# Edge units of an attention layer in two groups of three instead of three groups of two, one table set for exponential and logarithm, and a small chain of work spread over more groups

## The chip, the core and the metric

The kernel runs on one core of a Trainium2 chip. That core has TensorE (PE, matrix multiplication; its weight loads are listed as PEld), VectorE (DVE), ScalarE (ACT), GpSimd (POOL) and a queue engine (SP) that issues transfers. Each runs its own list of instructions in order, and they wait for one another on semaphores. The metric is the device time of one launch in microseconds (us).

## The reference

Four layers in a row on an input of 4 images of 16 x 16 places and 192 channels, all in 32-bit floating point. Layers 0 and 2 are attention blocks (normalise, windowed attention with relative positions, projection, normalise, two-layer perceptron with GELU). Layers 1 and 3 are spectral layers. Only the attention is touched here. Its core, for each window of 14 x 14 places:

```python
xp = pad(norm(x))                      # 16 x 16 -> 28 x 28, four windows per image
q, k, v = split(xp_windows @ qkv_w + qkv_b)          # 12 heads of 16 channels
attn = (q * scale) @ k.T + rel_h[..., :, None] + rel_w[..., None, :]
out = softmax(attn) @ v
out = (out @ proj_w + proj_b)[:, :16, :16]
```

Since 16 = 14 + 2, each image has one full window and three windows that consist mostly of padding. Only the 2-wide strips of them are real. Padded places have a zero input, so their keys are the bias of the key projection: a query in such a window sees its few real keys, and for all the padding three folded keys with a logarithm of a sum of exponentials as their weight.

## The kernel before

The two attention layers (l = 0 and 1 in the program) run the same code. The 12 heads are held in 3 slots of 4 heads. Places are in two kinds of groups:

- a *main* group is a slot and an image: 196 queries and 196 keys, the keys in two tiles of 128;
- an *edge* group is a slot and the strips of all images. The right strips (e = 0) and the lower strips (e = 1) are 120 queries each, with 120 real and 3 folded keys. A pair of slot and strip is called a unit here; there are six, and an edge group has two.

`GROUPS` (L254) lists 15 groups: 0 to 3 are slot 0 of the four images, 4 to 7 slot 1, 8 to 10 the edges of slots 0 to 2, and 11 to 14 slot 2 of the four images. The written order is a pipeline over them. In step n TensorE does, in interleaved quarters (loop at L1090),

- `turn(n)` (L1034): the scores of group n with keys on the partitions, heads 0 and 1 first (pair 0), then heads 2 and 3 (pair 1). ScalarE takes the exponential (`probsT`, L1398);
- `score(n + 2)` (L1006): the scores of a later group with queries on the partitions, from which VectorE takes each query's largest (`take_max`, L1585) and turns it (L1596); SP carries it by four transfers into the row of the relative positions that `turn` reads later;
- `weigh(n - 1)` (L1054) after half of pair 1: probabilities times values, with the sums of the probabilities.

`score(h)` waits until the largest of the half before last has been taken, because it writes the same banks. `turn(n)` waits for the exponentials of group n - 1 and for `pv_out` of group n - 2, since weighed results share bank 4 with the turned scores.

After the weighing, ScalarE copies the result out (`take_weighed`, L1385), which from the third group on waits until GpSimd has finished group n - 2 (the buffers are two deep). VectorE turns the sums and inverts them (`sum_up`, `spread`, L1606 to L1618; in its list two steps later), and GpSimd multiplies (`divide`, L808 to L821): for slot 2 straight to its place, for slot 0 by way of a part that is masked, for slot 1 by way of a mask and an addition. The edge results go to four pieces of the target, so each step of it is four instructions. `out_project` (L892) of image b waits for the division of group 11 + b (10 + b in the new numbering).

The folded keys' logarithms are made by a chain over three engines, which begins with the relative rows: VectorE turns them (`turn_rows`, L1624) and takes largest values (L1631); GpSimd subtracts (`shift_pads`, L785); ScalarE takes the exponential (L1403); VectorE adds up (L1637); ScalarE takes the logarithm (L1406); VectorE adds the largest back (`log_pads`, L1642); GpSimd fills three rows (`pad_rows`, L791); VectorE turns all back (L1647). GpSimd's own order is: edge inputs of slot 0, `shift_pads`, edge inputs of slot 1, `pad_rows`, then `divide(0)`, `divide(1)`, edge inputs of slot 2, `divide(2)` and on.

ScalarE holds one set of function tables at a time. A table load is its own instruction, before L1406 and again before the exponential that follows.

## Time and profile before

| | us |
|---|---|
| median of 3 runs (lowest to highest) | 334.32 (333.93 to 335.57) |
| the profiled execution | 337.13 |
| its span, first to last instruction | 335.3 |
| PE busy | 319.6 (95%) |
| PEld busy | 239.4 (71%) |
| DVE busy | 190.3 (57%) |
| ACT busy | 143.7 (43%) |
| POOL busy | 102.0 (30%) |
| mean granted TensorE clock | 0.98 of full |

```profile
PEclk9599998999999999999999999799999999999999
```

### The profile page before, as it was taken

What the parts mean: (1) busy time and instruction counts of PE and PEld (TensorE: products, weight loads), DVE (VectorE), ACT (ScalarE), POOL (GpSimd) and SP (SyncE); (2) the same over time, 40 slices, a digit from 0 to 9 for tenths busy, and PEclk for the clock granted to TensorE, in tenths of its full rate; (3) what the DMA queues carried; (4) which work ended last, traced back from release to release, by engine and by line L of the source; (5) the groups of instructions that cost most, each with busy time, mean ns of one, the idle gap of its engine ahead of it and who ended that gap; (6) DMA issues with size and microseconds to landing.
All of it is one profiled execution on the core that took longest, in us unless ns stands there. A gap on an engine that the chain in (4) does not pass through costs nothing.

```text
span 335.3 us, 9323 instructions
## 1 busy us (share of the span) xinstructions
PE 319.6 (95%) x3886; PEld 239.4 (71%) x3886; DVE 190.3 (57%) x457; ACT 143.7 (43%) x312; POOL 102.0 (30%) x215
## 2 busy tenths in 40 slices
PE   6999997999998999999999999799999899999997
PEld 3447686887876439977855769578887644998576
DVE  4473784877867400136674578587785920335572
ACT  3277136554556522024247515655455455002430
POOL 3000553487551049100000066277663104000000
PEclk9599998999999999999999999799999999999999
DMA  7973000000031103020021100000000000000002
GB/s 203 383 269 68 15 7 16 8 10 5 5 86 43 25 0 118 2 70 2 0 96 20 37 4 12 14 9 6 5 4 3 3 0 0 2 0 2 0 2 94
DMA packets 10268, 13.81 MB, mean 41 GB/s; under 512 B 3505, under 2 KB 8337, under 8 KB 10226
## 3 DMA queue, kind: packets, MB, share of 16 engines
q1 hardware_dynamic: 9602, 13.12, 12.5%
q8 instruction: 31, 0.51, 0.7%
q10 hardware_dynamic: 624, 0.09, 0.2%
q14 instruction: 11, 0.09, 0.1%
HBM read 10.95 MB, written 0.79 MB: 35 GB/s over the span
## 4 chain that ended last, share of the span: by engine, by line
PE 86%; DVE 7%; ACT 4%; DMA 2%; issue 1%; ACTq 0%; DVEq 0%
PE banks L1034 13%; PE banks L1006 12%; PE banks L1128 10%; PE banks L1146 9%; PE banks L962 6%; PE banks L1054 6%; PE banks L925 6%; PE banks L896 3%; PE banks L1312 2%; PE banks L885 2%; PE banks L1159 2%; PE banks L1206 2%; PE banks L938 2%; DMA slot_cols<-in_slot_cols 2%; ACT arena L1398 1%; PE banks L1176 1%
## 5 line engine op out<-in xcount | busy, mean ns | idle before, releaser
L1398 ACT ACTIVATE arena<-banks 128x392 f32<-128x392 f32 (+1 forms) x120 | 50.0, 469 | 44.0 <-PE banks L1034 44.0
L1585 DVE TENSOR_REDUCE negmax<-banks 128x4 f32<-128x784 f32 (+1 forms) x52 | 46.7, 897 | 17.5 <-PE banks L1006 17.0
L1006 PE MATMUL banks<-attention_arena 32*128 32x196 f32 x384 | 50.7, 365 | 0.9 <-DVE negmax L1581 0.4
L1034 PE MATMUL banks<-attention_arena 32*128 32x196 f32 x384 | 48.8, 351 | 0.4 <-ACT arena L1398 0.4
L1034 PE MATMUL banks<-attention_arena,keys 32*128 32x196 f32 x384 | 45.7, 332 | 0.0
L1006 PE MATMUL banks<-keys,attention_arena 32*128 32x196 f32 x384 | 45.5, 331 | 0.0
L1034 PEld LDWEIGHTS banks<-attention_arena 32*128 32x128 f32 x384 | 31.5, 191 | 7.0 <-issue 5.2
L1128 PE MATMUL banks<-yT,fc 128*128 128x512 f32 (+1 forms) x96 | 33.3, 607 | 0.0
L1006 PEld LDWEIGHTS banks<-keys,attention_arena 32*128 32x128 f32 x384 | 33.0, 190 | 0.0
L1034 PEld LDWEIGHTS banks<-attention_arena,keys 32*128 32x128 f32 x384 | 33.0, 190 | 0.0
L1006 PEld LDWEIGHTS banks<-attention_arena 32*128 32x128 f32 x384 | 29.9, 190 | 3.7 <-DVE negmax L1581 1.9
L1146 PEld LDWEIGHTS banks<-fc,arena 128*128 128x128 f32 x192 | 31.1, 190 | 1.5 <-ACT arena L1418 1.5
L756 POOL COPY edge_rel<-attention_arena 128x64 f32<-128x64 f32 (+1 forms) x24 | 4.3, 236 | 91.5 <-DVE attention_arena L1571 91.5
L1146 PE MATMUL banks<-fc,arena 128*128 128x192 f32 x192 | 31.7, 327 | 0.0
L1687 DVE TENSOR_TENSOR x_tok<-banks,x_plus_bias 128x384 f32<-128x384 f32 x8 | 4.5, 558 | 46.2 <-PE banks L1146 46.2
L1054 PE MATMUL banks<-arena,v_and_ones 128*32 128x196 f32 (+1 forms) x480 | 25.2, 328 | 4.7 <-ACT arena L1398 4.6
L1128 PEld LDWEIGHTS banks<-yT,fc 128*128 128x128 f32 (+1 forms) x96 | 12.8, 188 | 17.9 <-issue 15.4
L925 PE MATMUL banks<-yT,qkv 128*128 128x512 f32 (+1 forms) x48 | 21.6, 675 | 1.0 <-DVE yT L1504 1.0
L1054 PEld LDWEIGHTS banks<-arena,v_and_ones 128*32 128x32 f32 (+1 forms) x480 | 12.2, 109 | 13.4 <-ACT arena L1398 9.1
L962 PE MATMUL banks<-attention_arena,rel 32*32 32x192 f32 x512 | 21.2, 321 | 0.0
L1418 ACT ACTIVATE arena<-banks,cols 128x512 f32<-128x512 f32 x24 | 14.7, 687 | 14.9 <-PE banks L1128 14.9
L811 POOL TENSOR_TENSOR divided_part<-o_and_sums,inverse_sums 128x196 f32<-128x196 f32 (+1 forms) x20 | 12.4, 620 | 26.2 <-DVE inverse_sums L1618 26.2
(181 smaller groups left out, 583.2 us busy)
## 6 DMA issues: line engine op xcount, KB each, us to landing
fc<-in_fc SPq DMA_DIRECT2D x2, 768.0 KB, 5.0
fc<-in_fc SPq DMA_DIRECT2D x2, 576.0 KB, 5.6
attention_arena<-negmaxT SPq DMA_DIRECT2D x68, 1.0 KB
rel<-in_rel SPq DMA_DIRECT2D x2, 448.0 KB, 5.9
x_tok<-in_x SPq DMA_DIRECT2D x4, 192.0 KB, 4.4
inverse<-in_inverse SPq DMA_DIRECT2D x1, 768.0 KB
inverse<-in_space_back SPq DMA_DIRECT2D x1, 768.0 KB, 3.9
qkv<-in_qkv SPq DMA_DIRECT2D x1, 576.0 KB, 3.8
```

The lines of the kernel that those rows point to most:

```text
L811: pool.tensor_tensor(part, o, inverse, ALU.mult).then_inc(s.divided, 1)
L896: last = mm(m.bank[out_bank(b)][:, CH * tile:CH * (tile + 1)], m.oT[:, part, at:at + 128], wl["proj"][:, part], start=part == 0, stop=part ...
L925: ins = mm(bank[:, :], wl["qkv"][rows, half, 128 * g:128 * (g + 1)], m.yT[rows, half, 512 * part:512 * (part + 1)], start=not short, stop= ...
L962: ins = mm(bank[row(quad), 192 * n:192 * (n + 1)], wl["rel"][row(quad), 0 if kind == "rel_h" else 1, at % WIN], q[:, :, :, at], start=True ...
L1006: ins = mm(o, asking, asked, start=not with_rel, stop=bool(with_rel))
L1034: last = mm(m.bank[4 + j][key_rows(b), cols * tile:cols * (tile + 1)], keys_of(slot, b, j, tile)[with_rel], queries_of(slot, b, j, tile)[w ...
L1054: last = mm(m.bank[weighed_in(n)][row(j), out_at], values_of(slot, b, j, tile), m.probsT[key_rows(b), n % P_RING, j, cols * tile:cols * (t ...
L1128: ins = mm(m.bank[j % 8][:, :], wl["fc1"][rows, half, 128 * hid:128 * (hid + 1)], m.yT[rows, half, 512 * g:512 * (g + 1)], start=not short ...
L1146: last = mm(m.bank[4 + b][:, CH * tile:CH * (tile + 1)], m.hidT[:, hid, at:at + 128], wl["fc2"][:, hid], start=hid == 0, stop=hid == HID_T ...
L1398: run(m.probsT[keys, n % P_RING, j, 0:cols], m.bank[4 + j][keys, 0:cols], ACT.Exp).then_inc(s.probs, 1)
L1418: run(m.hidT[:, hid, 512 * g:512 * (g + 1)], m.bank[j % 8][:, :], ACT.Gelu, bias=wl["cols"][:, hid:hid + 1])\
L1585: dve.tensor_reduce(at[rows, 4 * part:4 * part + 4].rearrange("k (j a) -> k j a", a=2), m.banks[rows, 2 * part:2 * part + 2, 0:2 * keys].r ...
```

## The change

Line numbers of the new kernel are 26 to 53 higher. There are four parts.

1. The six units are in two edge groups of three (`PER_GROUP`): slot 0 both strips and slot 1 right strip; slot 1 lower strip and slot 2 both strips. There are 14 groups; 8 and 9 are edges. An edge group has 6 steps of `turn` and of `score` where it had 4, exponentials of 360 columns where it had 240, 12 multiplications in `weigh` where it had 8. All buffers for it grow to three units.
2. ScalarE loads one named table set after L1370's work, in which both exponential and logarithm are; no load stands around the logarithm.
3. The folded keys' chain moves in the written order. On VectorE `turn_rows` and the largest come after `take_max(5)`, the sums after `take_max(9)`, `log_pads` after `take_max(11)`, the turn back to step 4. On ScalarE its exponential follows group 1 (it followed group 0), and the logarithm group 2 (it followed group 1). GpSimd's order is as it was.
4. The semaphore of two small loads at the start is split: TensorE's first transposes wait for `ident` alone, not for `slot_cols` too.

```diff
-PAD_BLOCKS = SLOTS * 2 * 4
+UNITS = 2 * SLOTS
+PER_GROUP = 3
+PAD_BLOCKS = UNITS * 4
-GROUPS += [(slot, EDGES) for slot in range(SLOTS)]
+GROUPS += [(third, EDGES) for third in range(UNITS // PER_GROUP)]
+def units(n):
+    return range(PER_GROUP * GROUPS[n][0], PER_GROUP * (GROUPS[n][0] + 1))
+def key_tiles(b):
+    return 2 if b < EDGES else PER_GROUP
+def steps_of_group(n):
+    return 2 * key_tiles(GROUPS[n][1])
...
+                def divide_edges(n, ring):
+                    o, part, inverse = by_units(m.o[:, ring]), by_units(m.part[:, ring]), by_units(m.inverse[:, ring])
                     pool.tensor_tensor(part, o, inverse, ALU.mult).then_inc(s.divided, 1)
                     pool.wait_ge(s.divided, divided(n))
+                    for at, u in enumerate(units(n)):
+                        slot, e = divmod(u, 2)
+                        if slot == 1:
+                            ins = pool.tensor_scalar(part[:, at], part[:, at], masked(slot), None, ALU.mult)
+                            continue
+                        for to, of in zip(pieces(m.oT[:, slot // 2], e), in_pieces(part[:, at], e)):
+                            ins = pool.tensor_scalar(to, of, masked(slot), None, ALU.mult)
+                    ins.then_inc(s.divided, 1)
                     pool.wait_ge(s.divided, divided(n) + 1)
+                    at, u = [(at, u) for at, u in enumerate(units(n)) if unit_slot(u) == 1][0]
+                    for to, of in zip(pieces(m.oT[:, 0], u % 2), in_pieces(part[:, at], u % 2)):
                         ins = pool.tensor_tensor(to, to, of, ALU.add)
                     ins.then_inc(s.weighed, 1)
...
                         for q in range(4):
-                            turn(l, n, 0, quarter(STEPS, q))
+                            turn(l, n, 0, quarter(steps_of_group(n), q))
                             score(l, h, quarter(steps_of(h), q))
...
-                    pe.wait_ge(ident_loaded, 16 * 2)
+                    pe.wait_ge(ident_loaded, 16)
...
-                        load_table(ACT.Exp)
+                        act.preload_act_table_set("natural_log_exp_and_others")
...
-                    if n == 0:
+                    if n == 1:
                         act.wait_ge(edge_rows, edge_row(l, "shifted"))
                         run(m.padexp[:], m.padexp[:], ACT.Exp, scale=4.0).then_inc(edge_rows, 1)
-                    elif n == 1:
+                    elif n == 2:
                         act.wait_ge(edge_rows, edge_row(l, "summed"))
                         run(m.padlog[:], m.padsum[:], ACT.Ln).then_inc(edge_rows, 1)
...
-                turn_rows()
                 take_max(2 * FIRST)
-                take_pad_max()
                 for n in range(N_GROUPS):
-                    if n == 1:
-                        sum_pads()
-                    elif n == 2:
-                        log_pads()
-                    elif n == 3:
+                    if n == 4:
                         turn_rows_back()
                     if n + AHEAD < N_GROUPS:
                         take_max(2 * (n + AHEAD) + 1)
+                        if n == 0:
+                            turn_rows()
+                            take_pad_max()
+                        elif n == 2:
+                            sum_pads()
+                        elif n == 3:
+                            log_pads()
                         if n >= 2:
                             invert(n - 2)
```

The order of instructions on VectorE around the folded keys' chain, before. `negmax` is the largest of a half group (`take_max(4)` is the first), `negmaxT` its turned copy, `edge_rel` the relative rows, `o_turned`, `recip` and `inverse_sums` the inverted sums of group 0:

```order
L1624 STREAM_TRANSPOSE edge_rel_turned<-edge_rel 128x768
L1585 TENSOR_REDUCE negmax<-banks 128x4
L1631 TENSOR_REDUCE pad_max<-edge_rel_turned 128x48 x2
L1585 TENSOR_REDUCE negmax<-banks 128x4
L1596 STREAM_TRANSPOSE negmaxT<-negmax 128x32
L1585 TENSOR_REDUCE negmax<-banks 128x4
L1637 TENSOR_REDUCE pad_sum<-pad_exp 128x48 x2
L1585 TENSOR_REDUCE negmax<-banks 128x4
L1596 STREAM_TRANSPOSE negmaxT<-negmax 128x32
L1585 TENSOR_REDUCE negmax<-banks 128x4
L1642 SCALAR_TENSOR_TENSOR pad_log<-pad_max,pad_log 128x96
L1585 TENSOR_REDUCE negmax<-banks 128x4
```

And now:

```order
L1630 TENSOR_REDUCE negmax<-banks 128x4 x2
L1641 STREAM_TRANSPOSE negmaxT<-negmax 128x32
L1676 STREAM_TRANSPOSE edge_rel_turned<-edge_rel 128x768
L1683 TENSOR_REDUCE pad_max<-edge_rel_turned 128x48 x2
L1630 TENSOR_REDUCE negmax<-banks 128x4 x2
L1641 STREAM_TRANSPOSE negmaxT<-negmax 128x32
L1630 TENSOR_REDUCE negmax<-banks 128x4 x2
L1641 STREAM_TRANSPOSE negmaxT<-negmax 128x32
L1689 TENSOR_REDUCE pad_sum<-pad_exp 128x48 x2
L1651 STREAM_TRANSPOSE o_turned<-o_and_sums 128x224
L1655 RECIPROCAL recip<-o_turned 128x7
L1670 STREAM_TRANSPOSE inverse_sums<-recip 128x224
```

The turn of the relative rows and the largest of the pads moved behind the second and before the third `take_max`; the sums moved from before the fourth to behind the sixth, just ahead of the inversion for group 0.

Further on in VectorE's list now, from the inversion of group 0 to that of group 1:

```order
L1670 STREAM_TRANSPOSE inverse_sums<-recip 128x224
L1630 TENSOR_REDUCE negmax<-banks 128x4 x2
L1641 STREAM_TRANSPOSE negmaxT<-negmax 128x32
L1694 SCALAR_TENSOR_TENSOR pad_log<-pad_max,pad_log 128x96
L1651 STREAM_TRANSPOSE o_turned<-o_and_sums 128x224
L1655 RECIPROCAL recip<-o_turned 128x7
L1670 STREAM_TRANSPOSE inverse_sums<-recip 128x224
```

The row L1694 (`log_pads`, L1642 before, which stood ahead of the inversion of group 0) is two `take_max` and a `negmaxT` behind that inversion.

The division of the edge groups on GpSimd, before (from group 8 into group 10; targets of four pieces):

```order
L811 TENSOR_TENSOR divided_part<-o_and_sums,inverse_sums 128x240
L815 TENSOR_SCALAR attention_arena<-divided_part,slot_cols 128x32x2
L815 TENSOR_SCALAR attention_arena<-divided_part,slot_cols 128x2x14x2
L815 TENSOR_SCALAR attention_arena<-divided_part,slot_cols 128x2x2x14
L815 TENSOR_SCALAR attention_arena<-divided_part,slot_cols 128x2x32
L811 TENSOR_TENSOR divided_part<-o_and_sums,inverse_sums 128x240
L818 TENSOR_SCALAR divided_part<-divided_part,slot_cols 128x240
L821 TENSOR_TENSOR attention_arena<-attention_arena,divided_part 128x32x2
L821 TENSOR_TENSOR attention_arena<-attention_arena,divided_part 128x2x14x2
L821 TENSOR_TENSOR attention_arena<-attention_arena,divided_part 128x2x2x14
L821 TENSOR_TENSOR attention_arena<-attention_arena,divided_part 128x2x32
L808 TENSOR_TENSOR attention_arena<-o_and_sums,inverse_sums 128x32x2
```

And now (all of group 8, and the first half of group 9):

```order
L848 TENSOR_TENSOR divided_part<-o_and_sums,inverse_sums 128x3x120
L856 TENSOR_SCALAR attention_arena<-divided_part,slot_cols 128x32x2
L856 TENSOR_SCALAR attention_arena<-divided_part,slot_cols 128x2x14x2
L856 TENSOR_SCALAR attention_arena<-divided_part,slot_cols 128x2x2x14
L856 TENSOR_SCALAR attention_arena<-divided_part,slot_cols 128x2x32
L853 TENSOR_SCALAR divided_part<-divided_part,slot_cols 128x120
L861 TENSOR_TENSOR attention_arena<-attention_arena,divided_part 128x32x2
L861 TENSOR_TENSOR attention_arena<-attention_arena,divided_part 128x2x14x2
L848 TENSOR_TENSOR divided_part<-o_and_sums,inverse_sums 128x3x120
L853 TENSOR_SCALAR divided_part<-divided_part,slot_cols 128x120
L856 TENSOR_SCALAR attention_arena<-divided_part,slot_cols 128x32x2
L856 TENSOR_SCALAR attention_arena<-divided_part,slot_cols 128x2x14x2
```

Every edge group now has the masked copies (L856) of two units, and the mask (L853) and the additions (L861) of a third; the four direct products of slot 2 (L808) are gone.

On TensorE, between two weighings of step 9 and 10 before:

```order
L1034 MATMUL banks<-edge_q,edge_k 123x120 x2
L1006 MATMUL banks<-attention_arena 128x196 x2
L1034 MATMUL banks<-edge_rel,edge_keys 123x120 x2
L1006 MATMUL banks<-keys,attention_arena 128x196 x2
L1034 MATMUL banks<-edge_q,edge_k 123x120 x2
L1006 MATMUL banks<-attention_arena 128x196 x2
L1034 MATMUL banks<-edge_rel,edge_keys 123x120 x2
L1006 MATMUL banks<-keys,attention_arena 128x196 x2
L1054 MATMUL banks<-arena,v_and_ones 32x120 x8
```

And now, the weighing with three units, and what follows it up to the end of the edge group's turn:

```order
L1095 MATMUL banks<-arena,v_and_ones 32x120 x12
L1075 MATMUL banks<-edge_rel,edge_keys 123x120 x2
L1075 MATMUL banks<-edge_q,edge_k 123x120 x2
L1047 MATMUL banks<-attention_arena 128x196 x2
L1075 MATMUL banks<-edge_rel,edge_keys 123x120 x2
L1047 MATMUL banks<-keys,attention_arena 128x196 x2
L1075 MATMUL banks<-attention_arena 128x196 x2
L1047 MATMUL banks<-attention_arena 128x196 x2
```

Six steps of an edge `turn` stand against four of a main `score`, so that two of its steps come before one of the other's in every second quarter.

## Rows read from the trace of the kernel before

**Rows 1.** Busy us (xcount) of PE, PEld, DVE, ACT, POOL, then PEclk; groups 3 to 8.

```profile
64.81:83.24 18.43, 18.43 (x404) 15.29 (x408) 13.46 (x31) 9.92 (x26) 15.51 (x26) 1.00 0.04 7
```

**Rows 2.** The same view: TensorE idle in layer 0, and after it in both layers.

```profile
53.40:55.60 2.20, 0.00 (x0) 0.00 (x0) 1.67 (x5) 2.16 (x5) 0.60 (x3) 1.00 0.11 26
56.20:59.50 3.30, 3.30 (x44) 2.88 (x40) 1.08 (x3) 1.22 (x3) 1.37 (x2) 0.50 0.02 5
...
213.20:216.50 3.30, 3.30 (x44) 2.69 (x40) 0.93 (x2) 1.18 (x3) 1.38 (x2) 0.50 0.02 5
```

**Rows 3.** Chain of waits, layer 0, groups 0 to 2: start us, us, what.

```profile
49.54 0.80 PE banks L1054 x16
...
52.18 1.28 ACT L1406
...
53.78 1.28 ACT L1398
...
55.62 1.07 PE banks L1054 x16
...
60.98 0.84 PE banks L1054 x16
```

**Rows 4.** The same chain later: weighing of groups 3 and 8, first output projection.

```profile
64.81 0.80 PE banks L1054 x16
...
83.24 0.55 PE banks L1054 x16
...
98.03 1.50 PE banks L896 x8
```

**Rows 5.** Timeline of VectorE, layer 0: start us, us, engine line op out<-in xcount.

```profile
43.27 0.97 DVE L1624 STREAM_TRANSPOSE edge_rel_turned<-edge_rel 128x768 f32<-128x768 f32 x1
...
45.44 0.90 DVE L1631 TENSOR_REDUCE pad_max<-edge_rel_turned 128x48 f32<-128x96 f32 x2
46.26 0.96 DVE L1585 TENSOR_REDUCE negmax<-banks 128x4 f32<-128x784 f32 x1
...
47.40 0.93 DVE L1585 TENSOR_REDUCE negmax<-banks 128x4 f32<-128x784 f32 x1
48.81 0.91 DVE L1637 TENSOR_REDUCE pad_sum<-pad_exp 128x48 f32<-128x96 f32 x2 [0.48 <-ACT pad_exp L1403]
```

**Rows 6.** Timeline of GpSimd, layer 0: pad rows and division of group 0.

```profile
54.13 0.60 POOL L791 TENSOR_TENSOR edge_rel_turned<-pad_log 128x24 f32<-128x24 f32 x3 [2.52 <-DVE pad_log L1642]
56.32 0.60 POOL L811 TENSOR_TENSOR divided_part<-o_and_sums,inverse_sums 128x196 f32<-128x196 f32 x1 [1.59 <-DVE inverse_sums L1618]
57.01 0.78 POOL L815 TENSOR_SCALAR attention_arena<-divided_part,slot_cols 128x196 f32<-128x196 f32 x1
```

**Rows 7.** Timeline of GpSimd, layer 0: division of groups 8 to 11.

```profile
88.58 0.69 POOL L811 TENSOR_TENSOR divided_part<-o_and_sums,inverse_sums 128x240 f32<-128x240 f32 x1 [1.43 <-DVE inverse_sums L1618]
89.38 1.65 POOL L815 TENSOR_SCALAR attention_arena<-divided_part,slot_cols 128x64 f32<-128x64 f32 x4
...
92.93 0.89 POOL L818 TENSOR_SCALAR divided_part<-divided_part,slot_cols 128x240 f32<-128x240 f32 x1
93.90 1.12 POOL L821 TENSOR_TENSOR attention_arena<-attention_arena,divided_part 128x64 f32<-128x64 f32 x4
...
97.13 0.62 POOL L808 TENSOR_TENSOR attention_arena<-o_and_sums,inverse_sums 128x196 f32<-128x196 f32 x1 [0.24 <-DVE inverse_sums L1618]
```

**Rows 8.** Timeline of VectorE: first turn for the sums of group 8.

```profile
87.39 0.40 DVE L1606 STREAM_TRANSPOSE o_turned<-o_and_sums 128x256 f32<-128x256 f32 x1
```

**Rows 9.** Groups by line and shape, 43 to 110 us: busy us, mean ns.

```profile
L1006 PE MATMUL banks<-attention_arena 32*128 32x196 f32 x160 | 23.0, 364 | 0.0
...
L1034 PE MATMUL banks<-edge_q,edge_k 32*123 32x120 f32 x48 | 5.1, 284 | 0.0
```

**Rows 10.** Timeline of the start: normalised input and its first transposes.

```profile
6.22 0.98 ACT L1337 ACTIVATE normed<-x_tok,norm_shift,rstd 128x192 f32<-128x192 f32 x2 [0.44 <-DVE norm_shift L1526]
...
6.95 1.09 PE L885 MATMUL banks<-ident,normed 128*128 128x128 f32 x8 [1.51 <-DMA slot_cols<-in_slot_cols]
```

More of the change, by code:

```diff
@@ L359, in divided @@
 def divided(n):
-    return sum((1, 2, 0)[slot] for slot, _ in GROUPS[:n]) + 1
+    return sum((1, 2, 0)[slot] if b < EDGES else 2 for slot, b in GROUPS[:n]) + 1
 def max_landed(n):
@@ L799, in divide @@
-                    o, part, inverse = m.o[:, ring, 0:cols], m.part[:, ring, 0:cols], m.inverse[:, ring, 0:cols]
-                    if b < EDGES:
-                        places = [inner(m.oT[:, slot // 2])[:, b]]
-                        split = lambda ap: [ap.rearrange("k (r w) -> k r w", r=WIN)]
-                    else:
-                        places = [p for e in range(2) for p in pieces(m.oT[:, slot // 2], e)]
-                        split = lambda ap: [p for e in range(2) for p in in_pieces(ap[:, EDGE_REAL * e:EDGE_REAL * (e + 1)], e)]
+                    if b == EDGES:
+                        divide_edges(n, ring)
+                        return
@@ L806, in divide @@
+                    dst, shape = inner(m.oT[:, slot // 2])[:, b], lambda ap: ap[:, 0:MAIN_KEYS].rearrange("k (r w) -> k r w", r=WIN)
+                    o, part = shape(m.o[:, ring]), shape(m.part[:, ring])
                     if slot == 2:
-                        for to, of, by in zip(places, split(o), split(inverse)):
-                            ins = pool.tensor_tensor(to, of, by, ALU.mult)
-                        ins.then_inc(s.weighed, 1)
+                        pool.tensor_tensor(dst, o, shape(m.inverse[:, ring]), ALU.mult).then_inc(s.weighed, 1)
@@ L810, in divide @@
                         return
+                    pool.tensor_tensor(part, o, shape(m.inverse[:, ring]), ALU.mult).then_inc(s.divided, 1)
+                    pool.wait_ge(s.divided, divided(n))
+                    if slot == 0:
+                        pool.tensor_scalar(dst, part, masked(slot), None, ALU.mult).then_inc(s.weighed, 1)
+                        return
+                    pool.tensor_scalar(part, part, masked(slot), None, ALU.mult).then_inc(s.divided, 1)
+                    pool.wait_ge(s.divided, divided(n) + 1)
@@ L1102, in attention @@
                     else:
-                        turn(l, n, None, range(STEPS))
+                        turn(l, n, None, range(steps_of_group(n)))
                         weigh(l, n - 1)
@@ L1607, in sum_up @@
                     dve.wait_ge(s.inverted, sums_turned(n))
-                    dve.reciprocal(m.recip[:, ring, 0:wide], m.turned[:, ring, 0:cols].rearrange("k (n c) -> k n c", c=GROUP)[:, :, HD * (1 - VALUE_HALF[slot])])\
-                       .then_inc(s.inverted, 1)
+                    turned = m.turned[:, ring, 0:cols].rearrange("k (n c) -> k n c", c=GROUP)
+                    if b < EDGES:
+                        dve.reciprocal(m.recip[:, ring, 0:wide], turned[:, :, HD * (1 - VALUE_HALF[slot])]).then_inc(s.inverted, 1)
+                        return
+                    for half in range(2):
+                        own = [at for at, u in enumerate(units(n)) if VALUE_HALF[unit_slot(u)] == half]
+                        at = slice(4 * own[0], 4 * own[-1] + 4)
+                        ins = dve.reciprocal(m.recip[:, ring, at], turned[:, at, HD * (1 - half)])
+                    ins.then_inc(s.inverted, 1)
                 def spread(n):
```

140 lines of the change are left out of this document (75 added, 65 removed).

## The prediction

> **What bounds the kernel now.** I read the page first: TensorE is busy 95% of the span, the others far less. Then the stages of an attention layer: from the weighing of group 3 to that of group 8 TensorE has no idle time at all, at full clock, and the weighings of main groups follow one another about every 3.65 us [rows 1, 4]. So in the steady part a group costs its matrix work, and one group fewer would be worth a step. The exception stands in the chain of waits at groups 1 and 2 [rows 3]: the second half of group 1's weighing chain goes over ScalarE, which loads a table at 52.18, takes the logarithm, loads a table again at 53.78, and only then takes the exponential that the weighing at 55.62 waits for. TensorE does nothing from 53.3 to 55.6, and then runs at 0.50 of its clock for 3.4 us [rows 2]. Layer 1 shows the same. Last I read the timelines of VectorE and GpSimd around the two places where the change moves their work [rows 5 to 8]; the reader should see there how long each link of a chain is, since neither engine is the bound by its sum.
>
> A step n below is one round of the loop; the weighing of group n - 1 falls into it.
>
> **The tables (a gain, certain).** Two loads of 1.28 us and the logarithm leave the place between the exponentials of groups 1 and 2. The idle 2.3 us goes, and with it the cause of the low clock, whose 3.4 us at half speed cost 1.7 us. That is 4.0 us per layer. Without it group 3 would be weighed at 64.81 - 4.0 = 60.8.
>
> The first load ends at 53.46 and the second begins at 53.78 [rows 3], so that 0.32 us holds the logarithm and every drain around it. The Trainium skill, ScalarE: Activation LUTs, section "What ACT_TABLE_LOAD costs", puts a switch at about 2.66 us, drain included. By that rule two switches would be worth 5.3 us per layer, 2.7 us more than the rows; the rows decide.
>
> **The folded keys' chain, first place (a loss).** Before, VectorE turned the relative rows at 43.27 in a pause and took the pads' largest at 45.44 while it waited for scores [rows 5]. Both now stand ahead of `take_max(6)`. The scores for `take_max(5)` are there at 46.26 at the latest, when VectorE came free of the pads' largest; I take 45.9, an estimate. So: 45.9 + 0.96, negmaxT 0.2, turn 0.97, largest 0.90, `take_max(6)` 0.93 gives 49.95, where it ended at 48.33. `score(8)` waits for it, and behind that TensorE's whole list. Some 0.2 to 0.3 of the 1.6 is slack: a loss of 1.3 us, weighing of group 0 at 50.9. The pads' exponential (0.76) now lies ahead of the exponentials of group 2, where these wait about as long for TensorE: nothing, and 0.7 if I misjudge that.
>
> **Second place (a loss).** `log_pads` is now behind `take_max(11)`, and GpSimd's `pad_rows` stands ahead of `divide(0)`. `take_weighed(2)` waits for `divide(0)`, and `turn(4)` waits for that. Follow VectorE: `take_max(9)` can start at 53.8 (one weighing of 0.8 and two half steps after the first loss) and ends at 54.8, negmaxT 55.0, sums 55.9 [rows 5], inversion of group 0 57.0, `take_max(10)` 57.95, `take_max(11)` 58.9, negmaxT 59.1, `log_pads` 59.4. Then GpSimd [rows 6]: pad rows 0.60, division 0.60 + 0.78 with 0.3 between them, 61.65; the copy out 0.33, 62.0. TensorE would be ready for `turn(4)` at 59.85: it idles 2.2 us. Together the front keeps -4.0 + 1.3 + 2.2 = -0.5 us per layer, group 3 weighed at 64.3. Bounds: -1.5 (both stalls a third shorter) to 0.
>
> **The edge groups on TensorE.** The number of multiplications stays. Half a group's step is (3.65 - 0.80) / 2 = 1.4 us of scores. Its main stream has four steps, so 0.33 to 0.36 each (a multiplication stands at 364 ns, overlap included [rows 9]). An edge multiplication has 120 columns for 196, so 0.36 x 120/196 = 0.22: the edge stream takes 4 x 0.22 = 0.9 before and 6 x 0.22 = 1.3 now (rows 9's 284 ns holds overlap with its neighbours). So three units fit under a main group, on paper. Two steps of the edge's come first in every second quarter, which starts the main stream 0.2 later; six such segments per layer give 1.2 at most, and nothing if the streams run freely as in rows 9's stretch, where the edge stream runs ahead. The step in which `score(10)` met `turn(8)`, both edges, lasted as long as the others because of the exponentials, and becomes a main one. I take +0.7 per layer up to the weighing of group 8, between 0 and 1.4.
>
> One step less is worth 3.65, less 0.5 for four more multiplications in two weighings: 3.1 us per layer. I don't book it, for this reason:
>
> **GpSimd at the end of the groups (takes the saved step back).** Before, from the weighing of group 8 (83.24) to the first output projection (98.03) it is 14.8 us, TensorE working throughout [rows 4]. The projection waits for the division of the first group of slot 2. The division of group 8 started at 88.58, 5.35 after its weighing. Now that start comes later by 0.2 (longer weighing), 0.2 (segments), and 0.3 to 0.4 (a second reciprocal, and turns half as long again as the 0.40 of rows 8): 6.1. A division of three units costs, by rows 7: the product of 360 columns 0.97 (0.60 for 196, 0.69 for 240), four masked copies 1.65, the mask of one unit 0.5 (0.89 for 240 columns, 0.78 for 196), two additions 0.56, waits 0.2: 3.9 us. It was 2.5, 2.9 and 1.1. Two of them in a row, then 0.62 + 0.1 for the main group: 6.1 + 7.9 + 0.7 + 0.1 = 14.8. The projection comes exactly as late after group 8 as before, though TensorE is done 3 us earlier: it idles those 3 us. ScalarE is held too, since `take_weighed(11)` waits for `divide(9)`. Book 0, between -1.0 and +0.7.
>
> **Start.** TensorE waited for `slot_cols` until 6.95. The last normalised tile is ready at 7.20 [rows 10], so the transposes end at about 7.65, not 8.04: 0.4 less, of which half may be lost in the low clock that follows: -0.3, between -0.4 and 0.
>
> **Clock.** Idle stretches of 2.3 us were followed by 3.4 us at 1.2 GHz in both layers [rows 2]. Now there are a stretch of 3.0 us at the end and one of 2.2 in front of `turn(4)`, in each layer. After the one at the end part of the low stretch falls on waits for VectorE: 1.4 us. After the other 1.7 us. I expect the first in both layers (4 in 5), the other is as likely as not.
>
> **The sum.** Per layer -0.5 + 0.7 + 0 = +0.2; both layers +0.4, start -0.3: +0.1. The clock at the end of both layers +2.8, and a fair part of the rest: I take +3.1 in all, against the profiled execution 337.13 -> 340.2. That execution is 2.8 above the median of the runs; I carry the difference over: 334.3 + 3.2 = 337.5.
>
> **Rivals.**
> - *The stalls come, the clock doesn't fall.* For: 2.2 and 3.0 us are idle in all, and it is not shown what split of idle and work lowers the clock. Against: 2.3 did it twice. +0.1: 334.4.
> - *GpSimd is not what ends last.* The saved step stays, if the divisions overlap more than their rows say or start earlier. For: GpSimd is busy only 30%. Against: its rows at this place are back to back with 0.1 between [rows 7]. 2 x -3.1 + 0.1 + 1.7 (front clock once) = -4.4: 330.
> - *Neither GpSimd nor VectorE's order matters*, as the change's parts suggest: -4.0 - 3.1 + 0.7 per layer, -0.3: -13: 321. Against: the waits are in the list.
> - *Strict order on TensorE costs all of it.* Segments at 1.4 per layer, all four clock falls (6.2), front at 0: +8.7: 343. In the rows nothing shows it, since four edge steps stand there against four main ones.
>
> TensorE: Matmul & The Clock Gate, section "Step-by-step: what each phase is for", in the Trainium skill says that matrix multiplications stay in program order and only weight loads are pulled forward. By that rule the full 0.2 per segment would be paid, +0.5 per layer over my value; the rows of before, with four steps against four, can't show it.
>
> **How the numbers follow.** Forecast 0.50 (336 to 341), no clock fall 0.14, GpSimd not last 0.18, everything gained 0.08, order on TensorE 0.10. What a measurement of this kernel can tell from no change is 0.5%, 1.7 us: 332.6 to 336.0. Faster: 0.18 + 0.08 + 0.03 of the second case = 0.29. Same: 0.11 of that case and 0.06 of the forecast's = 0.17. Slower: 0.54. The range reaches from 329 (most of the GpSimd rival) to 342.
>
> **What would show it.** In the profile after: VectorE's `take_max(6)` of layer 0 ends at about 50; the idle time before `turn(4)` is near 2 us and its releaser ScalarE's copy, which waited for GpSimd; no table load stands among the exponentials; each edge division lasts 3.9 us; TensorE idles 3 us before the first output projection, released by GpSimd; the clock is at 0.5 after it. If TensorE doesn't idle at either place, the forecast is wrong; if it does, and the clock stays at 1.0, it is 3 us too high.

## The result: a little slower, about as forecast

| | us |
|---|---|
| before, median of 4 runs (lowest to highest) | 334.12 (331.76 to 335.57) |
| after, median of 4 runs | 338.00 (337.29 to 341.31) |
| ratio of the runs, after to before | 1.0129 (1.0067 to 1.0192) |
| the same in a second series (12 runs of after: 333.94 to 341.29, median 337.12) | 1.0044 (1.0012 to 1.0076) |
| profiled execution after (before 337.13) | 338.66 |
| its span after | 336.9 |
| PE busy after | 315.7 (94%) |
| mean granted TensorE clock after | 0.995 |

337.5 was forecast. In both series the whole interval lies above 1; in size the ratios say +4.3 and +1.5 us. Ratios compare runs in the same state, so that of the second series leaves out its two slowest runs (341.22 and 341.29); by its medians it is 337.12 for 334.17, +3.0. The strip of granted clock of the profile after has no slice at 5 now and one at 7, late in the second attention layer:

```profile
PEclk9999999999999999999999999999997999999999
```

The profile answers the forecast's steps one after the other. First what TensorE waited for in the attention layers, after (us in total, times, longest):

```profile
PE banks L937 <- POOL attention_arena L834: 5.3, 2, 2.7
...
PE banks L1075 <- issue: 2.7, 2, 1.3
PE banks L1047 <- DVE negmax L1630: 2.0, 2, 1.0
```

The wait of 4.6 us for ScalarE's exponentials is gone. In its place stand three waits, each once per layer. The first output projection waits for GpSimd. The turn of group 4 waits for something that its record doesn't name ("issue"). And `score(8)` waits for VectorE's largest, which is the first place of the moves (in layer 0 this wait ends at 49.70). The chain of waits after, layer 0 (start us, us, what), answers to [rows 3, 4]:

```profile
50.63 0.80 PE banks L1095 x16
...
58.73 0.80 PE banks L1095 x16
...
60.41 1.33 issue
...
64.01 0.80 PE banks L1095 x16
...
83.25 0.76 PE banks L1095 x24
...
97.82 1.54 PE banks L937 x8
```

Group 0 is weighed at 50.63 (49.54 before), group 2 at 58.73 (60.98), group 3 at 64.01 (64.81), group 8 at 83.25 (83.24). The projection starts at 97.82 (98.03), though it is behind one group less.

VectorE, ScalarE and GpSimd in front of `turn(4)`, from their timelines after (start us, us, engine line op, x; in brackets the idle time before and its releaser), answer to [rows 5, 6]:

```profile
46.88 0.94 DVE L1676 STREAM_TRANSPOSE edge_rel_turned<-edge_rel 128x768 f32<-128x768 f32 x1
47.85 0.91 DVE L1683 TENSOR_REDUCE pad_max<-edge_rel_turned 128x48 f32<-128x96 f32 x2
48.68 1.85 DVE L1630 TENSOR_REDUCE negmax<-banks 128x4 f32<-128x784 f32 x2
...
53.80 0.97 DVE L1630 TENSOR_REDUCE negmax<-banks 128x4 f32<-128x784 f32 x1 [0.37 <-PE banks L1047]
...
58.86 0.22 DVE L1694 SCALAR_TENSOR_TENSOR pad_log<-pad_max,pad_log 128x96 f32<-128x96 f32 x1
```

```profile
59.16 0.63 POOL L817 TENSOR_TENSOR edge_rel_turned<-pad_log 128x24 f32<-128x24 f32 x3 [5.13 <-DVE pad_log L1694]
59.73 0.61 POOL L836 TENSOR_TENSOR divided_part<-o_and_sums,inverse_sums 128x196 f32<-128x196 f32 x1
60.44 0.78 POOL L839 TENSOR_SCALAR attention_arena<-divided_part,slot_cols 128x196 f32<-128x196 f32 x1
```

```profile
61.31 0.33 ACT L1427 ACTIVATE o_and_sums<-banks 128x196 f32<-128x196 f32 x1 [2.93 <-POOL attention_arena L839]
```

Read them as one chain. The turn of the relative rows and the pads' largest (46.88 and 47.85) stand between `take_max(5)` and `take_max(6)`. Further on the logarithms come at 58.86, GpSimd fills the pad rows and divides group 0 until 61.2, ScalarE's copy of group 2, which waited 2.93 us for it, runs at 61.31, and TensorE goes on at 61.74. The "issue" of 1.33 us in the chain of waits is taken to be this wait: TensorE goes on 0.1 us after the copy's end, and the kernels with the chain at its old places have no such wait.

GpSimd at the end of the groups, after, answers to [rows 7]:

```profile
89.22 0.95 POOL L848 TENSOR_TENSOR divided_part<-o_and_sums,inverse_sums 128x360 f32<-128x360 f32 x1 [2.20 <-DVE inverse_sums L1670]
90.27 1.65 POOL L856 TENSOR_SCALAR attention_arena<-divided_part,slot_cols 128x64 f32<-128x64 f32 x4
91.88 0.59 POOL L853 TENSOR_SCALAR divided_part<-divided_part,slot_cols 128x120 f32<-128x120 f32 x1
92.56 0.58 POOL L861 TENSOR_TENSOR attention_arena<-attention_arena,divided_part 128x64 f32<-128x64 f32 x2
93.21 0.95 POOL L848 TENSOR_TENSOR divided_part<-o_and_sums,inverse_sums 128x360 f32<-128x360 f32 x1
...
97.08 0.60 POOL L834 TENSOR_TENSOR attention_arena<-o_and_sums,inverse_sums 128x196 f32<-128x196 f32 x1
```

From 89.22 to 97.68 GpSimd never waits. An edge division takes 3.9 us (89.22 to 93.14). Busy time by stretch, after (columns as in [rows 1]):

```profile
64.01:83.25 19.24, 19.24 (x465) 16.35 (x468) 15.30 (x31) 10.62 (x26) 14.67 (x23) 1.00 0.03 7
83.25:97.82 14.57, 11.73 (x245) 9.64 (x245) 9.44 (x23) 7.14 (x17) 9.96 (x20) 1.00 0.19 65
256.30:259.60 3.30, 3.30 (x35) 2.62 (x33) 1.18 (x3) 0.00 (x0) 0.43 (x1) 0.53 0.00 0
```

The first row is groups 3 to 8: 19.24 us for 18.43 before [rows 1], TensorE working throughout. The second is the stretch from which a step was saved: 14.57 us, nearly as before (14.79, 98.03 less 83.24), with 2.84 of it idle. The third is the low clock behind the wait of layer 1; layer 0 has none.

### The profile page after: what moved, and what is told of

It reads as the page before. It is cut to its first block, busy times and chain, and to the rows that moved or that the text cites. A ratio compares the mean times of both kernels' runs of the same rounds, so it can differ in the third digit from the quotient of the medians.

```text
span 336.9 us, 9270 instructions
## 1 busy us (share of the span) xinstructions
PE 315.7 (94%) x3886; PEld 235.6 (70%) x3886; DVE 189.5 (56%) x449; ACT 136.4 (40%) x296; POOL 104.3 (31%) x217
## 4 chain that ended last, share of the span: by engine, by line
PE 78%; DVE 13%; POOL 4%; issue 2%; DMA 1%; ACT 1%; DVEq 0%
PE banks L1047 10%; PE banks L1169 10%; PE banks L1187 9%; PE banks L1075 9%; PE banks L1003 6%; PE banks L966 5%; PE banks L1095 5%; DVE negmax L1630 3%; PE banks L937 3%; PE banks L926 2%; PE banks L1353 2%; PE banks L1200 2%; PE banks L1247 2%; PE banks L979 2%; POOL attention_arena L856 1%
## 5 line engine op out<-in xcount | busy, mean ns | idle before, releaser
L1442 ACT ACTIVATE arena<-banks 128x392 f32<-128x392 f32 (+1 forms) x112 | 49.1, 491 | 42.7 <-PE banks L1075 42.7
L1630 DVE TENSOR_REDUCE negmax<-banks 128x4 f32<-128x784 f32 (+1 forms) x48 | 45.9, 962 | 18.6 <-PE banks L1047 18.4
L1047 PE MATMUL banks<-attention_arena 32*128 32x196 f32 x384 | 49.3, 356 | 3.0 <-DVE negmax L1630 2.0
L1075 PE MATMUL banks<-attention_arena 32*128 32x196 f32 x384 | 47.7, 348 | 3.0 <-issue 2.7
L1047 PE MATMUL banks<-keys,attention_arena 32*128 32x196 f32 x384 | 44.1, 323 | 0.0
L1075 PEld LDWEIGHTS banks<-attention_arena 32*128 32x128 f32 x384 | 30.7, 189 | 9.9 <-issue 8.5
L1047 PEld LDWEIGHTS banks<-attention_arena 32*128 32x128 f32 x384 | 28.1, 183 | 6.9 <-DVE negmax L1630 3.3
L1075 PEld LDWEIGHTS banks<-attention_arena,keys 32*128 32x128 f32 x384 | 32.3, 190 | 0.0
L1047 PEld LDWEIGHTS banks<-keys,attention_arena 32*128 32x128 f32 x384 | 31.7, 184 | 0.0
L1095 PE MATMUL banks<-arena,v_and_ones 128*32 128x196 f32 (+1 forms) x480 | 24.3, 323 | 0.0
L1003 PEld LDWEIGHTS banks<-attention_arena,rel 32*32 32x32 f32 x512 | 15.8, 105 | 5.1 <-issue 0.4
L1615 DVE TENSOR_TENSOR attention_arena<-banks,attention_arena 128x384 f32<-128x384 f32 x16 | 11.9, 861 | 12.6 <-PE banks L1003 12.6
```

The source lines that it names most:

```text
L1003: ins = mm(bank[row(quad), 192 * n:192 * (n + 1)], wl["rel"][row(quad), 0 if kind == "rel_h" else 1, at % WIN], q[:, :, :, at], start=True ...
L1047: ins = mm(o, asking, asked, start=not with_rel, stop=bool(with_rel))
L1075: last = mm(m.bank[4 + j][key_rows(b), cols * tile:cols * (tile + 1)], keys_of(n, j, tile)[with_rel], queries_of(n, j, tile)[with_rel], st ...
L1095: last = mm(m.bank[weighed_in(n)][row(j), out_at], values_of(n, j, tile), m.probsT[key_rows(b), n % P_RING, j, cols * tile:cols * (tile + 1)],
L1442: run(m.probsT[keys, n % P_RING, j, 0:cols], m.bank[4 + j][keys, 0:cols], ACT.Exp).then_inc(s.probs, 1)
L1615: ins = dve.tensor_tensor(at, bank[:, 0:2 * 192].rearrange("k (w n) -> k w n", w=2), at, ALU.add)
```

## The experiments

Twelve runs were made, eleven new kernels and the changed one again. Ratios are to the kernel before in the same series, with 95% intervals; its median was 335.4, 335.3 and 334.2 us in the three series. Since the start of a run varies by 3 us (last section), stages are compared within one profile: from the start of the long projection behind the second eight transposes (its row is x18; 15.78 before) to a weighing.

### The parts of the front

**one_table**: the kernel before, with

```diff
-                        load_table(ACT.Exp)
+                        act.preload_act_table_set("natural_log_exp_and_others")
```

> The kernel before with one change: the table set with both functions, nothing else. Theory A (the forecast's term): the idle 2.3 us and the 1.7 us of low clock go in each layer, group 3 is weighed 4.0 us earlier than before (60.8), and nothing else is late: 334.1 - 8.0 = 326.1, between 325 and 328. Rival B (only the idle time goes; the clock falls all the same, at another place): 334.1 - 4.6 = 329.5. Rival C (the chain for the folded keys is late next and takes the place of the loads): 332 or more.

326.82 us, ratio 0.9791 (0.9758 to 0.9825), 7.0 us by the ratio, where theory A had 8.0, rival B 4.6 and rival C 2 at most. **table_moved** is that and the chain's new places (the diff has VectorE's; ScalarE's two parts move likewise, to groups 1 and 2):

```diff
-                turn_rows()
                 take_max(2 * FIRST)
-                take_pad_max()
...
                         take_max(2 * (n + AHEAD) + 1)
+                        if n == 0:
+                            turn_rows()
+                            take_pad_max()
+                        elif n == 2:
+                            sum_pads()
+                        elif n == 3:
+                            log_pads()
```

> The kernel before with the table set and with the folded keys' chain at its new places, still 15 groups with two units in an edge group. Theory A: the moves cost 3.4 us per layer (1.1 to 1.3 in front of take_max(6), 2 in front of turn(4)), so the front keeps only 0.6 us per layer of the 4.0: 334.1 - 1.2 = 332.9, and 6 to 7 us more than the kernel with the table set alone. It also has the late divide(0), so that TensorE waits before turn(4). Rival D (the moves cost nothing, what is lost is lost by the groups of three): the same time as with the table set alone, 326.

333.81 us, 0.9987 (0.9955 to 1.0019). The chains of waits of the two, layer 0 (the rows are the long projection, then weighings; of table_moved also the wait in front of `turn(4)`), first one_table:

```profile
12.54 6.59 PE banks L925 x18
46.30 0.81 PE banks L1054 x16
...
53.88 0.80 PE banks L1054 x16
57.78 0.81 PE banks L1054 x16
```

```profile
14.05 6.59 PE banks L925 x18
49.13 0.80 PE banks L1054 x16
57.23 0.81 PE banks L1054 x16
58.91 1.31 issue
62.49 0.81 PE banks L1054 x16
```

Group 0 is weighed 33.76 us behind the projection's start in the one, 35.08 in the other: 1.3 us for the first place. From group 0 to group 3 it is 11.48 and 13.36: 1.9 us for the second. Against the kernel before (64.81 less 15.78, 49.03) the table set alone has 45.24, 3.8 us less. So the moves give back 3.2 of 3.8 us per layer, and rival D is out.

**old_places**: the changed kernel with the chain back (the reverse of the diff above, and ScalarE's two parts after groups 0 and 1).

> The changed kernel with the folded keys' chain back at the places it had before (turn of the rows ahead of take_max(4), largest behind it, sums ahead of take_max(7), logarithms ahead of take_max(9); ScalarE's parts after groups 0 and 1). Groups of three, table set and start stay. Theory A: 3.4 us per layer come back, group 3 of layer 0 weighed at 60.6: 338.0 - 6.8 = 331.2. Rival D (moves cost nothing): 338. Rival E (the chain's parts lie in pauses only by chance, half comes back): 334.5.

331.52 us, 0.9902 (0.9867 to 0.9937). Theory A again: group 3 is weighed 45.40 us behind the projection's start (61.17 less 15.77), where the changed kernel has 48.47 (64.01 less 15.54). With groups of three the moves cost 3.1 us, as with groups of two.

**start_only**: the kernel before with the semaphore split. **one_table_start**: that and the table set.

> The kernel before with the semaphore of the two small loads split, nothing else. Theory A: the first transposes begin 0.3 us earlier and the projection behind them is held by its weights: 334.1 - 0.3 = 333.8, no difference that can be told. Rival F (the shorter idle time keeps the clock up from 8.4 to 15.2 us, and that is worth time): -2 to -3, 331.5.

> The kernel before with the table set and the split semaphore, 15 groups, chain as before: the two parts that cost nothing elsewhere. Theory A: 326.8 - 0.3 = 326.5, and 1.5 to 2 us above the kernel with groups of three whose division is not waited for. Rival (the start alone was worth 1.2 us, as its own run had it): 325.6.

333.64 us, 0.9964 (0.9931 to 0.9998), and 328.12 us, 0.9801 (0.9774 to 0.9829), where the table set alone had 0.9791. The first says 1.2 us, the second nothing. The second is 1.6 us above its expectation; its profile had a slow start (last section). The split's 0.3 us is not told from nothing.

The profile of start_only shows something else. TensorE idles 2.3 us in front of group 1's weighing in both layers, as before, but in its layer 0 the granted clock stays at 1.00 behind that:

```profile
15.27 6.59 PE banks L926 x18
...
62.87 0.80 PE banks L1055 x16
```

Group 3 comes 47.60 us behind the projection's start, where it is 49.03 with the low clock (before) and 45.24 without the loads (one_table). So the low clock cost 1.4 us of the 3.8, and the loads and the logarithm themselves 2.4.

### The groups of three

**groups_only**: the changed kernel with the old table loads, the chain's old places, and

```diff
                     pe.wait_ge(ident_loaded, 16)
+                    pe.wait_ge(columns_loaded, 16)
```

> The kernel before with the groups of three alone: 14 groups, two table loads around the logarithm, the chain and the start as before. Theory A: the mixed segments cost 0.8 us per layer, the saved step of 3 us is lost in the wait for GpSimd in front of the first output projection (2.6 us idle), and the clock falls behind that wait in about every second layer (1.6 us): +0.8 x 2 + 1.6 = +3.2, 338. Rival (the groups of three are worth something, and the table set and the moves get in their way): below the time of before by 2 or more, 332.

338.27 us, 1.0100 (1.0053 to 1.0147). Alone, the groups of three cost 3.3 us (0.0100 x 334.2), as theory A had it. Its profile has both waits, once per layer, and behind three of the four the clock is at half; two such stretches, both of layer 0 (columns as in [rows 1]):

```profile
PE banks L937 <- POOL attention_arena L834: 5.3, 2, 2.7
PE banks L1095 <- ACT arena L1443: 4.6, 2, 2.3
```

```profile
54.00:57.00 3.00, 3.00 (x44) 3.00 (x40) 1.86 (x2) 0.89 (x2) 0.54 (x1) 0.50 0.03 9
96.00:101.00 5.00, 5.00 (x40) 4.24 (x38) 1.41 (x4) 0.00 (x0) 0.60 (x1) 0.50 0.02 5
```

**after_again**: the changed kernel unaltered.

> The changed kernel once more, unaltered, for a narrower ratio to the kernel before than four runs gave. Theory A (the terms as the profiles show them: +0.3 us per layer, the clock at the end of every second layer +1.6, start -0.3): ratio 1.005 to 1.013, 336 to 338. Against the kernel with the short division, -1.2 per layer and fewer falls of the clock: 3 to 4 us more than that. Rival (the first measurement stood high by chance): ratio 1.000.

337.12 us, 1.0044 (1.0012 to 1.0076): just under the expected 1.005 to 1.013. Half of its runs are between 333.9 and 337.1.

**short_division**: the changed kernel; slot 2's two units of group 9 go straight to their places.

```diff
-                    pool.tensor_tensor(part, o, inverse, ALU.mult).then_inc(s.divided, 1)
+                    direct = [unit_slot(u) == SLOTS - 1 for u in units(n)]
+                    shared = PER_GROUP - sum(direct)
+                    pool.tensor_tensor(part[:, 0:shared], o[:, 0:shared], inverse[:, 0:shared], ALU.mult).then_inc(s.divided, 1)
+                    for at, u in enumerate(units(n)):
+                        if direct[at]:
+                            for to, of, by in zip(pieces(m.oT[:, 1], u % 2), in_pieces(o[:, at], u % 2), in_pieces(inverse[:, at], u % 2)):
+                                pool.tensor_tensor(to, of, by, ALU.mult)
...
+                        if direct[at]:
+                            continue
```

> The changed kernel; in the division of group 9 the two units of slot 2 are multiplied straight to their places, as slot 2 was before, so that the product and the mask take only the one unit of slot 1. Theory A (GpSimd's two edge divisions in a row are what the first output projection waits for): the division of group 9 takes 2.7 us instead of 3.9, the wait before the projection falls from 2.6 to 1.4 us, 1.2 us per layer: 338.0 - 2.4 = 335.6, perhaps another 1 us if the clock falls less often behind the shorter wait. Rival G (TensorE would be held by something else at that place, VectorE's largest or ScalarE's copy): the time stays at 338.

**early_inversion**: the changed kernel; the sums of groups 8 and 9 are inverted one `take_max` earlier in VectorE's list.

```diff
+EARLY = (8, 9)
...
+                    if n - 2 in EARLY:
+                        invert(n - 2)
                     if n + AHEAD < N_GROUPS:
                         take_max(2 * (n + AHEAD) + 1)
-                        if n >= 2:
+                        if n >= 2 and n - 2 not in EARLY:
                             invert(n - 2)
```

> The changed kernel; VectorE inverts the sums of the edge groups 8 and 9 one take_max earlier. Theory A: GpSimd's first edge division, which started at 89.22, starts at about 87.45, all behind it is 1.8 us earlier, and the wait before the projection falls from 2.6 to 0.8 us: 338.0 - 3.6 = 334.4, another 1 us if the clock falls less often. Rival H (take_max(25) and take_max(27), now 0.9 and 1.4 us later, hold TensorE as long as is won): 337.5.

333.35 us, 0.9979 (0.9939 to 1.0019), and 332.12 us, 0.9922 (0.9883 to 0.9962). The waits of TensorE at the projection, of short_division and then of early_inversion (2 layers):

```profile
PE banks L945 <- POOL attention_arena L834: 3.0, 2, 1.5
```

```profile
PE banks L938 <- POOL attention_arena L835: 1.8, 2, 0.9
```

5.3 us became 3.0 and 1.8, as theory A had it (2 x 1.4 and 2 x 0.8). By the ratios, against the second series of the changed kernel, that is 2.2 and 4.1 us. The medians lie 2 us lower than expected. In part that is the base, 338.0, which the second series puts lower; and in neither profile does the clock fall behind the shorter waits. Rivals G and H are out.

**old_short_early**: the changed kernel with the old places, the short division and the early inversion.

> The changed kernel with three edits at once: the folded keys' chain at its old places, the short division of group 9, the early inversion of groups 8 and 9. Theory A: 331.5 (old places alone) less the whole wait before the projection (2.6 us per layer) less the low clock that followed it in about every second layer (1.6 us): 331.5 - 5.2 - 1.6 = 324.7; TensorE waits for GpSimd at no place. If groups of three were worth a saved step then, it must beat the kernel of before with one table set (326.8). Rival I (what groups of three cost is TensorE's own time in the mixed segments, more than the 0.8 us per layer that the steps showed): 327 to 329.

324.83 us, 0.9720 (0.9658 to 0.9782). No wait for GpSimd is left. For the first time a kernel with groups of three is below the best one with groups of two (one_table, 0.9791), but the two intervals overlap, and they are of two series. The profiles tell the two apart. From one long projection to that of the next attention layer, first old_short_early, then one_table (12.66 and 12.54 are the starts):

```profile
164.57 6.59 PE banks L975 x18
```

```profile
166.22 6.59 PE banks L925 x18
```

That is 151.9 us for 153.7, 1.8 less per layer.

**best_quarters** is that kernel with the edge's steps dealt otherwise:

```diff
-    return range(-(-steps * q // 4), -(-steps * (q + 1) // 4))
+    return range(steps * q // 4, steps * (q + 1) // 4)
```

> The kernel with the three edits, and an edge group's six steps dealt to the quarters as 1, 2, 1, 2 instead of 2, 1, 2, 1. Rival order (strict program order on TensorE: two edge steps ahead of a main one delay it by 0.2 us): the segments lose their 0.8 us per layer, -1.6 in all. Theory A (half a step lasts as long as its longer stream, whatever the quarters): no change against the kernel with the three edits, within 0.5.

324.59 us, 0.9702 (0.9645 to 0.9759), not told apart from the one before. The weighings of groups 3 and 8, of old_short_early and then of best_quarters:

```profile
57.99 0.80 PE banks L1104 x16
...
77.44 0.76 PE banks L1104 x24
```

```profile
58.13 0.80 PE banks L1104 x16
...
77.20 0.77 PE banks L1104 x24
```

19.45 us became 19.07, where one_table has 18.67 (57.78 to 76.45). In layer 1 it is 19.36, 19.11 and 18.64. So a third to a half of the 0.8 us of the mixed segments hangs on which quarter has the extra step. The rival of order wanted all of it, theory A none; its "within 0.5" holds for the runs, which can't tell so little. What the rest is, no run shows. It doesn't follow the number of mixed quarters: in the changed kernel the step from the weighing of group 3 to that of group 4 takes 3.80 us for 3.65, though only its last part has edge scores in it, and the next, which has them throughout, 3.79 for 3.63 (3.88 in after_again).

**best_warm** is best_quarters with

```diff
-WARM_UPS = 3
+WARM_UPS = 4
```

> The best kernel so far (three edits, quarters 1, 2, 1, 2; 324.6) with four multiplications ahead of the first real work on TensorE instead of three, so that it is busy up to the first transposes. In some runs the first projection (six multiplications) takes 2.8 us, in others 4.3 to 5.5, and a low clock is recorded or the durations are twice as long. Theory K (the idle 1.0 to 1.5 us ahead of the transposes makes the clock fall in some runs): the slow starts go, median 323, lowest 322. Rival L (what the clock does at the start has nothing to do with this idle time): 324.6, or 0.5 more because the transposes start later.

321.89 us, 0.9622 (0.9596 to 0.9649), the fastest of all, and its four runs lie between 321.80 and 322.15. That is as theory K had it; what it doesn't prove stands in the last section.

## Why the prediction was right, step by step

- **Tables.** -4.0 per layer was forecast; 3.8 is measured in the profile of one_table, 7.0 us in the whole. Of the 3.8, 2.4 are idle time (2.3 forecast) and 1.4 the low clock (1.7 forecast), by start_only. The Trainium skill (ScalarE: Activation LUTs, section "What ACT_TABLE_LOAD costs") would have had 5.3 for the two switches alone; the rows' 2 x 1.28 was the better size.
- **First place.** +1.3 forecast, 1.3 measured. `take_max(6)` of layer 0 was to end at 49.95 and ended near 49.6 (48.68, the first of two of 0.93 each); group 0 was to be weighed at 50.9 and was at 50.63.
- **Second place.** +2.2 forecast, 1.9 measured. `take_max(9)` started at 53.80, as written (53.8); GpSimd's division ended at 61.2 (61.65), and TensorE went on at 61.74 (62.0). But only 1.3 us of it stands before `turn(4)`. The rest came in front of group 2's weighing: in one_table group 2 follows group 0 by 7.58 us, in table_moved by 8.10. The chain of waits of after goes over VectorE there (the sums and an inversion, then a largest at 56.88 that a `score` at 57.79 waited for). The forecast had one stall where there are two.
- **Front as a whole.** -0.5 forecast; group 3 at 64.01 for 64.81, less 0.24 for the earlier start, is -0.56.
- **Mixed segments.** +0.7 forecast, 0.81 in layer 0 and 0.74 in layer 1. The rule of strict order (the Trainium skill, TensorE: Matmul & The Clock Gate, section "Step-by-step: what each phase is for") would have had 1.2. best_quarters shows that order has a part in it, 0.4 us in layer 0 and 0.25 in layer 1.
- **GpSimd at the end.** This was the step that turned a gain into nothing, and it held nearly row by row: first edge division 6.1 us behind its weighing (5.97), 3.9 us each (3.92), the projection 14.8 us behind group 8 (14.57), 3.0 us idle (2.65 by the waits). short_division and early_inversion take it away in parts, old_short_early whole. ScalarE was held as well, as written: its copy at 97.21 waited 1.91 us for GpSimd's second edge division. The mask of one unit was put at 0.5 and took 0.59, which the sum of 3.9 doesn't feel.
- **Start.** -0.3 forecast; -0.24 in the profile (15.54 for 15.78), not told from nothing by runs. That it came near is luck. The transposes of one_table, table_moved and groups_only, which wait for both loads, begin at 6.59, 6.59 and 6.58, earlier than after (6.67). So the wait for `slot_cols` until 6.95 was, as far as these profiles show, a matter of that one execution. And the transposes took 1.94 us after, for 1.09 before.
- **Clock.** This term was mis-sized. +2.8 was booked for the low clock at the end of both layers. Of the falls in front only 0.2 was booked in the sum, though even odds on 1.7 in each layer would be 1.7. The profile after has it once, at the end of layer 1. From the first projection (L937) to the third it is 10.31 us in layer 0, from 97.82, and 11.49 in layer 1: 1.2 us for one fall. Behind the 1.3 us in front of `turn(4)` the clock never fell, in this profile or in the four others that have this wait. So the profiled execution came to 338.66 where 340.2 was forecast, 1.5 us less.
- **Carrying over.** The forecast took the profiled execution before, 2.8 us above the median, as that much high throughout. Its clock had been low three times, at the start and in both layers, for a mean of 0.98; its later runs have 0.99 to 1.00. The one after was only 0.7 above its median. The two errors, in the clock and here, nearly cancel: that 337.5 met 338.0 is partly luck. By the profiled executions the change costs 1.5 us, by the two series of runs 4.3 and 1.5.

Of the rivals, the stalls without a low clock (334.4) describes layer 0 of the profile after, and the runs at 334 in the second series; the range held both. GpSimd not last and everything gained are refuted by the rows at 93.21 and 97.08. Strict order costing all of it is refuted too, by 0.8 us per layer for its 1.4 and a front that kept 0.56. The kernel that has the saved step is old_short_early, with 1.8 us per layer less than one_table; 3.1 - 0.8 = 2.3 was to be expected.

## What to carry to other kernels

A step that is saved on the bounding engine can be worth nothing while a chain on an idle-looking engine (GpSimd, 31% busy) ends the stage: add up that engine's back-to-back rows from the last event that releases it to what waits for it. A small chain that is "spread over pauses" is paid at each place where its instruction stands ahead of one that the bounding engine waits for, so read for every moved instruction what is queued behind it, on each engine that it passes. Here one part of four gave 7 us alone, and two parts took it back. The table set and the groups of three, with the chain at its old places, a shorter division, an earlier inversion, other quarters and one more multiplication at the start, gave 12.6 us (0.0378 x 334.2).

## What the runs showed of the hardware

**The start is a lottery, and the granted clock on record does not always show it.** TensorE's first real work is eight transposes and six multiplications of the projection. From timelines (columns as above), first of after, then of early_inversion:

```profile
6.67 1.94 PE L926 MATMUL banks<-ident,normed 128*128 128x128 f32 x8 [0.89 <-DVE normed L1574]
9.60 5.07 PE L966 MATMUL banks<-yT,qkv 128*128 128x512 f32 x6 [1.00 <-DVE yT L1548]
```

```profile
6.75 1.07 PE L927 MATMUL banks<-ident,normed 128*128 128x128 f32 x8 [0.97 <-DVE normed L1575]
8.81 2.81 PE L967 MATMUL banks<-yT,qkv 128*128 128x512 f32 x6 [0.99 <-DVE yT L1549]
```

The same instructions take 1.8 times as long in the first, though its granted clock reads 1.00 there. A clock of 1.2 instead of 2.4 GHz for most of that time would make this; that the record misses it is inferred from the durations, not shown. Of the thirteen profiles with three multiplications ahead, four are like the first (after, after_again, old_places, start_only) and five like the second (one_table, groups_only, early_inversion, old_short_early, best_quarters). In four the projection took 4.3 to 5.5 us with a granted clock of 0.50 on record (before, table_moved, one_table_start, short_division). The long projection starts between 12.5 and 15.8, so it is worth up to 3 us. How long TensorE idles before the transposes, 0.8 to 1.5 us here, doesn't sort them: behind 1.47 us (old_short_early) and 0.80 (groups_only) they were at full speed, behind 0.83 (start_only) slow. With the fourth multiplication ahead (best_warm) the idle time is 0.55 us:

```profile
1.49 4.58 PE L1116 MATMUL banks<-arena 128*128 128x392 f32 x8 [1.49 <-DVE arena L1879]
6.62 1.08 PE L935 MATMUL banks<-ident,normed 128*128 128x128 f32 x8 [0.55 <-DVE normed L1583]
8.70 2.81 PE L975 MATMUL banks<-yT,qkv 128*128 128x512 f32 x6 [1.00 <-DVE yT L1557]
```

and the four runs stand within 0.35 us. One profile and four runs are few, and the edit changes two things: TensorE idles less and has worked longer before. Which of them keeps the start fast is not shown.

**An idle stretch of 2.3 to 2.7 us was followed by a low clock in some executions and not in others.** Behind the wait for GpSimd it fell in layer 1 but not in layer 0 of after, and in layer 0 but not in layer 1 of groups_only. Over all profiles there are 14 such stretches and 9 falls: 5 behind 6 waits for the loads, 4 behind 8 waits for GpSimd. Inside the attention layers, stretches of 1.5 us and under were followed by no fall in any profile here. What decides between the two stays open.
